# Second layer's vertical recursion on quarter arrays, and another strip order in the last layer

## Time and profile before

| | |
|---|---|
| time, 3 runs | 12891.12 us (12890.92 to 12896.08) |
| the profiled execution's own time | 12888.75 us |
| its span | 12887.0 us |
| PE busy | 12308.6 us (96%) |
| DVE, ACT, POOL busy | 8055.8, 5432.1, 4649.4 us |
| TensorE clock granted | 0.981 of full speed on average |
| layer 0, second stage, matmuls | 1371 to 2409 us |
| layer 1 vertical, matmuls | 2449 to 3776 us |
| layer 1 horizontal, matmuls | 3824 to 5154 us |
| layer 3, matmuls | 9649 to 12878 us |

### The profile page before, as it was taken

The page is one execution under the profiler, slowest core; times in us unless marked ns, Lnnn a source line. Parts: engine busy times, 40 slices in busy tenths (PEclk is TensorE's granted clock), DMA queues, the critical chain, the costliest instruction groups (busy, mean ns, idle before and its releaser), DMA issues. The chain is left out here.

```text
span 12887.0 us, 315788 instructions
## 1 busy us (share of the span) xinstructions
PE 12308.6 (96%) x126170; PEld 8518.5 (66%) x126170; DVE 8055.8 (63%) x17482; ACT 5432.1 (42%) x11157; POOL 4649.4 (36%) x3557
## 2 busy tenths in 40 slices
PE   7999999899989999899999999999989999999998
PEld 6877444577767777455555555555558887787777
DVE  0000677533335544688888888888877777777777
ACT  0000111211213333455555555555546766676666
POOL 0000222100000055566666666666643433334343
PEclk9999999999999999899999999999999999999999
DMA  4333456883765587666666666666642222222222
GB/s 127 135 131 132 132 152 160 158 158 70 153 125 157 151 211 206 94 89 87 88 88 89 87 88 89 88 88 88 89 88 49 50 55 49 52 54 51 52 52 47
DMA packets 2310007, 1323.92 MB, mean 103 GB/s; under 512 B 1872228, under 2 KB 2219867, under 8 KB 2222959
## 3 DMA queue, kind: packets, MB, share of 16 engines
q1 hardware_dynamic: 2041484, 1201.47, 47.0%
q10 hardware_dynamic: 267232, 104.65, 3.4%
HBM read 648.72 MB, written 450.74 MB: 85 GB/s over the span
## 5 line engine op out<-in xcount | busy, mean ns | idle before, releaser
L1583 PE MATMUL l_m<-l_wa,l_pix 128*128 128x288 f32 x8192 | 2211.5, 413 | 12.8 <-DMA l_left<-k_rim_dram 12.8
L1583 PEld LDWEIGHTS l_m<-l_wa,l_pix 128*128 128x128 f32 x8192 | 1475.5, 190 | 698.9 <-issue 375.4
L1439 POOL TENSOR_TENSOR l_qkv<-l_qkv,l_copies 128x576 f32<-128x576 f32 x1024 | 1437.4, 1404 | 633.6 <-DVE l_qkv L1775 633.6
L1429 POOL TENSOR_TENSOR l_pix<-l_raw 128x516 f32<-128x516 f32 x1024 | 1216.7, 1188 | 1043.6 <-DVE l_t L1812 1018.1
L1285 PE MATMUL l1h_ps<-l1h_ring,l1h_w 96*96 96x256 f32 x6120 | 1326.5, 379 | 51.2 <-ACT l1h_ring L1233 47.6
L1056 PE MATMUL l1v_ps<-l1v_rows,l1v_w 96*96 96x256 f32 x6120 | 1326.4, 378 | 31.1 <-ACT l1v_rows L1029 31.1
L2093 PEld LDWEIGHTS l_e<-k_ident,l_turn 128*112 128x112 f32 x9900 | 1086.3, 135 | 248.9 <-issue 126.0
L1285 PEld LDWEIGHTS l1h_ps<-l1h_ring,l1h_w 96*96 96x96 f32 x6120 | 998.6, 163 | 379.1 <-issue 48.0
L2093 PE MATMUL l_e<-k_ident,l_turn 128*112 128x128 f32 x9900 | 1164.3, 276 | 86.2 <-DVE l_out L2255 80.0
L1056 PEld LDWEIGHTS l1v_ps<-l1v_rows,l1v_w 96*96 96x96 f32 x6120 | 990.7, 162 | 366.5 <-issue 30.1
L1269 POOL TENSOR_TENSOR l1h_columns<-l1h_blocks,l1h_ring 96x2048 f32<-96x2048 f32 x64 | 356.2, 5588 | 2418.5 <-DVE l1h_ring L1318 2418.5
(11 more groups left out here) (245 smaller groups left out, 21890.5 us busy)
## 6 DMA issues: line engine op xcount, KB each, us to landing
l0a_x<-x_px_dram SPq DMA_DIRECT2D x128, 1176.0 KB, 5.1
l0b_x<-x_in_dram SPq DMA_DIRECT2D x128, 493.8 KB
l_raw<-l_raw SPq DMA_DIRECT2D x128, 483.6 KB, 7.2
l_raw<-x_dram SPq DMA_DIRECT2D x1280, 48.0 KB, 3.7
l_x<-x3p_dram SPq DMA_DIRECT2D x132, 384.0 KB
l_out<-x_dram SPq DMA_DIRECT2D x528, 96.0 KB
out_dram<-l_out SPq DMA_DIRECT2D x132, 384.0 KB
x_dram<-l0b_out ACTq DMA_DIRECT2D x256, 193.5 KB, 3.1
```

The source lines that it names most:

```text
L1429: nc.gpsimd.tensor_tensor(pix[:, n % 2, i, half * HALF:(half + 1) * HALF].rearrange("p (r w) -> p r w", w=PW), in0, in1, op).then_inc(pix_ ...
L1439: nc.gpsimd.tensor_tensor(q, q, copies[:, g % 2, 1:2, :].broadcast_to([128, 2, OUTC]), ALU.add)\
L1583: last = nc.tensor.matmul(bank[i][:, 0:OUTC], pix[:, k, i, first:first + 128], wa[:, b, i, :], start=True, stop=(i in (1, 2)))
```

## The change

1. **Layout.** `x1` is in natural column order (DVE's L910 and L916 write and read contiguously; ACT's copy reads 16 columns at a time).
2. **Vertical recursion.** A row of two images is kept in one of two layouts, by its parity. *Whole* (even rows): one image on partitions 0 to 47, the other on 64 to 111, 256 columns each. *Parted* (odd rows): the left column half of both images on partitions 0 to 47, the right half on 64 to 111, each half 130 columns wide, so that two columns are computed twice. A matmul takes its input from one side and writes to one side of PSUM, so a whole row gives a parted one and the reverse, with no copy. Each of the 5 taps is a 48x48 matrix, and per tap there are 4 matmuls, one for each quarter of the array, of 130 columns (from a whole row) or 128 (from a parted one). `ps[g]` has two banks, one for each input side. A step-group is thus 20 matmuls of the code in place of 3. DVE still does one instruction, on 112 partitions by 260 or 256 elements.
3. **Way up.** The result of row h is written over row h - 1 (`place`), so that layouts still alternate. At the turn ACT and POOL copy the last row into the whole layout, ten increments of `kept`, and PE waits for them.
4. **Copies and DMAs.** DVE and POOL clear the slots before the first load (8 and 4 of them). A chunk is loaded in 12 DMAs in place of 8 and saved in 4 in place of 4. On the way up ACT copies the whole rows and half of the parted ones, POOL the other half. The constants are loaded behind the first chunk.
5. **Layer 3.** POOL's strip copy (L2315) also waits until all four pieces of its unit are gated. With j = 1 DVE does piece 3 after the residuals.

```diff
@@ stage_l0_apply, DVE
-    place = out[:, kk, 2*n:2*n+2, 1:W+1].rearrange("p r (q u) -> p r u q", q=2)
+    place = out[:, kk, 2*n:2*n+2, 1:W+1]
@@ stage_l1_vertical
+    TAPS, HALO = 5, 2
+    RH = CH // 2
+    PART = HW2 + HALO
+    whole = sb("whole", [PP, SL, GI, RH, W + 2 * HALO])
+    parted = sb("parted", [PP, SL, GI, RH, 2, PART + 2 * HALO])
+    def place(n):  return n if n <= LAST else 2 * LAST - n - 1
+    def source(n): return n - 1 if n <= LAST else 2 * LAST - n
@@ tensor
     for n in range(1, STEPS + 1):
         for g in range(2):
...
+            elif n == LAST + 1:
+                pe.wait_ge(state[g], n - 1)
+                pe.wait_ge(kept, 10)
             else:
                 pe.wait_ge(state[g], n - 1)
-            for s in range(3):
-                last = nc.tensor.matmul(ps[g][0:C2, 0:GI * HW2], w[:, s, :],
-                    X[:, before // CH % SL, g*GI:(g+1)*GI, before % CH, s:s + HW2], start=(s == 0), stop=(s == 2))
-            last.then_inc(product[g], 1)
+            for t in range(TAPS):
+                for r in range(2):
+                    for c in range(2):
+                        if at % 2 == 0:
+                            first = t + c * (W - PART)
+                            x, width = whole[side(r), k, g, row, first:first + PART], PART
+                        else:
+                            first = t + 2 * r
+                            x, width = parted[side(r), k, g, row, c, first:first + HW2], HW2
+                        last = nc.tensor.matmul(ps[g][side(c), r, 0:width], w[side(r), t, :], x,
+                                                start=(t == 0), stop=(t == TAPS - 1), skip_group_check=True)
+                        if t == TAPS - 1:
+                            last.then_inc(product[g], 1)
@@ vector
-    dve.wait_ge(product[g], n)
+    dve.wait_ge(product[g], 4 * n)
     nc.vector.scalar_tensor_tensor(out=x, in0=ps[g][0:PP, :, 0:(HW2 if at >= 0 and at % 2 == 0 else PART)], ...
@@ gpsimd (new), way up
+    for g in range(2):
+        pool.wait_ge(state[g], up_step(c * CH))
+        for i in range(2):
+            for q in range(2):
+                turn_parted(nc.gpsimd.tensor_copy, c, 1, g, i, q).then_inc(turned_low, 1)
@@ stage_l3, DVE
                     if not (first and j == 0) and (j < 2 or last):
-                        for piece in (2, 3):
-                            gated(n if j else n - 1, j - 1 if j else 2, piece)
+                        gated(n if j else n - 1, j - 1 if j else 2, 2)
+                        if j != 1:
+                            gated(n if j else n - 1, j - 1 if j else 2, 3)
                     if j < 2 and not first:
                         for s in range(2):
                             residual(n, j, s)
+                    if j == 1:
+                        gated(n, 0, 3)
@@ stage_l3, POOL
                     pool.wait_ge(added, u + 1)
+                    pool.wait_ge(gate_out, u * 4 + 4)
                     nc.gpsimd.tensor_copy(strip[:, j], inner(4)).then_inc(saved, 1)
```

More of the change, by code:

```diff
@@ L916, in _ @@
                             nc.vector.tensor_tensor(
[L917 removed]
+                                place, bank[2 * n + 1][0:O, :].rearrange("p (r w) -> p r w", r=2), place,
                                 ALU.add).then_inc(added, 1)
@@ L998, in store_up @@
             def store_up(c):
                 k = c % 2
-                sp.wait_ge(turned, 2 * B * (NCH - c))
+                sp.wait_ge(turned, 12 * (NCH - c))
+                sp.wait_ge(turned_low, 8 * (NCH - c))
                 for i in range(B):
[L1002 to L1005, removed]
-                          .then_inc(stored[k], 16)
@@ L1019, in _, with rows_of_parted, turn_parted @@
             for k in range(2):
-                sp.wait_ge(stored[k], 128 * (NCH // 2))
+                sp.wait_ge(stored[k], 192 * (NCH // 2))
+        def rows_of_parted(c):
+            yield parted[:, c % SL, :, 0:RH - 1, :, :], HALO, slice(1, RH)
+            if c > 0:
+                yield parted[:, (c - 1) % SL, :, RH - 1:RH, :, :], HALO, slice(0, 1)
+            else:
+                yield keep[:].rearrange("p g (o i) w -> p g o i w", o=1), 0, slice(0, 1)
+        def turn_parted(copy, c, h, g, i, q):
+            for rows, margin, into in rows_of_parted(c):
+                first = margin + 2 * h
+                src = rows[side(h), g, :, i, first:first + HW2].rearrange("p v (n u q) -> p q n v u", n=WBLK // 2, q=2)
+                last = copy(turn_p[side(h), c % 2, g, i, :, q, into, :], src[:, q])
+            return last
@@ L1031, in _ @@
             for g in range(2):
                 act.wait_ge(state[g], LAST)
-                nc.scalar.activation(keep[:, g * GI:(g + 1) * GI, :],
-                                     X[:, SL - 1, g * GI:(g + 1) * GI, CH - 1, 1:HW2 + 1], ACT.Copy).then_inc(kept, 1)
+                for h in range(2):
+                    at = HALO + 2 * h
+                    copy(whole[side(h), SL - 1, g, RH - 1, HALO + h * HW2:HALO + (h + 1) * HW2],
+                         parted[side(h), SL - 1, g, RH - 1, h, at:at + HW2]).then_inc(kept, 1)
@@ L1035, in _ @@
+                copy(keep[:, g], parted[:, SL - 1, g, RH - 1, :, HALO:HALO + PART]).then_inc(kept, 1)
             for c in range(NCH - 1, -1, -1):
                 if c < NCH - 2:
[L1037 to L1043, removed]
+                    act.wait_ge(stored[c % 2], 192 * ((NCH - 1 - c) // 2))
@@ L1062, in _ @@
         @block.vector
         def _(dve):
[L1064 to L1068, removed]
+            nc.vector.memset(gn_w[:], 0.0)
+            nc.vector.memset(gn_p[:], 0.0)
+            for g in range(2):
+                last = nc.vector.memset(ps[g][32:HI, :, 0:PART], 0.0)
```

191 lines of the change are left out of this document (129 added, 62 removed).

## The result

The changed kernel takes 13168.26 us (median of 4 runs, 13157.29 to 13184.52) against 12891.02 us before: a ratio of 1.0217, 95% interval 1.0199 to 1.0234. It is 277 us slower, where 86 us faster was forecast. The profiled execution took 13184.52 us, its span is 13181.4 us.

A forecast was written before the change was run, and what follows sets the result against it. Vertical stage taken as bound by columns through PE, after the change by instruction packets. Terms -19 + 4 - 3 - 68 = -86 us; 12888.75 - 86 = 12803, the runs' median 2.4 above: 12805 us, range 12615 to 12950.

The forecast's parts named there:

- The vertical steps: Vertical stage: 319 instruction packets at 4.10 us each set the pace, 1307 us against 1326, so -19 us.
- DMA load doesn't seem to matter: Vertical stage: time per instruction packet taken as independent of DMA share: 4.24 us at 0.15, 4.37 at 0.02, 3.86 at 0.53.
- The price without load: PE's instruction stream, vertical stage: 4.10 us per packet of 256 instructions, bounds 3.86 and 4.45.
- the first rival: Vertical stage: instructions come in time and columns set the pace, -204 us there, kernel 12620 us; chance 0.15.
- The second rival: Vertical stage: instruction stream still slower with DMAs beside it, 4.77 us a packet, +128 us, kernel 13019 us; chance 0.12.
- DVE, ACT, POOL: Vertical stage: their work and DMA stay hidden behind PE's time, DVE's instruction 0.49 us, all at nothing.
- Edges: Vertical stage's start, turn and end: 0, +2 and +2, sum +4 us, bounds -3 and +12.
- Layer 0: DVE's add, made contiguous, may be 0.35 us shorter but off the path save at image ends: -3 us (0 to -6).
- Layer 3: With the strip copy after the fourth gate, the first gate takes 0.68 us, not 1.53: -68 us, bounds -90 and -20.
- the three terms: Layer 3, gain per unit: 0.83 us with j = 0, 0.25 with j = 1, 0 with j = 2.

The follow-up runs named there:

- the wait alone: The kernel before, with only the edit that makes POOL's strip copy in layer 3 wait for the gate's last pieces: 12748.88 us, ratio 0.9883.

## Why the prediction was wrong

- **The vertical steps** failed: forecast -19, bounds -95 and +93, measured +429. The count was right (319 packets). The failed step is "DMA load doesn't seem to matter". It rested on three stretches of 4 us in the earlier trace rows, the busiest at a share of 0.53, from a stage whose mean share is 0.23; the vertical stage stood at 0.66 in the earlier trace rows and at 0.90 in the last line of the earlier trace rows. I compared shares inside one quiet stage and carried the result to a busy one. The stage's own load was the thing to bound, and no row bounded it. In its place the runs show that the stage's transfers decide: 3.69 us a packet with the transfers cut, 5.5 with them, 8.8 at full input load.
- **The price without load** was too high, not too low: 3.69 us a packet against the 4.10 taken and the 3.86 called the lowest. I took layer 3's packets for a limit of delivery; they also had ACT, DVE and the wait for them in between, and how much of the 3.86 to 5.08 is which, no run separates. Without load the first rival, instructions in time, is nearly right: 12563.84 measured, 12620 worked out. That is closer than its terms: the stage took 1178 us against 1122, and layer 3 gained 153 us against 68.
- **The second rival** had the right mechanism, "with DMAs beside them", and 0.12 of the chance. It stopped at 4.77 us a packet, since its range was made of layer 3's 4.45 and 5.08; the stage went to 5.5.
- **The clock** had no term, in the stage or in layer 3. In the stage it is at most 200 of the 602 us.
- **The range** was added up wrong at its upper end: +93 + 4 - 3 - 20 on the median gives 12965, not 12950. The measured 13168 lies outside either.
- **DVE, ACT, POOL** hidden: right. DVE 484 and 489 ns, waiting for PE. **Edges** +10 against +4, inside the bounds. **Layer 0** -4 against -3: DVE's add fell from 1073 to 691 ns, 0.38 us where 0.35 was expected, and it was hidden, as said.
- **Layer 3** had the right mechanism and half the size: -140 against -68, outside its bounds of -90 and -20. The gates fell to 681 ns as forecast. Cut at each unit's first convolution matmul, the units with j = 0, 1, 2 took 1033.6, 914.9 and 1239.4 us in all before and 959.6, 872.4 and 1217.7 us in the changed kernel: 1.12, 0.64 and 0.33 us a slab, 2.1 in all, where the forecast had 0.83, 0.25 and 0. So each of the three terms was too small. With j = 0 the median unit gained 0.86 us, as forecast, and the mean more: these units spent 75 us at half clock before and 7 now. With j = 1, I gave 0.25 us, since DVE would wait for the projection. DVE in fact comes to that residual late because its gates were slow, as the wait alone shows by shortening the residual's wait by 33 us. With j = 2, I had 0; 12 of its 22 us are shorter waits of PE, mostly for "issue", and why is open.
- The Trainium skill's rule for such pairs ("SBUF — State Buffer", "SBUF: two separate sides") is that a DVE instruction with two SBUF inputs and a GpSimd one that reads SBUF take the shared ports in turn, whole instructions at a time. 894 against 682 ns with the copy moved agrees in the main. By the rule, a gate that starts 0.05 us after a copy of 1.04 us would end 1.67 us after its start, an estimate from the earlier trace rows and that rule; it took 1.53.
- "Mostly hidden", as the Trainium skill has instruction fetching ("Runtime: NRT & Kernel Launch", "Instruction fetch mechanics"), holds here without transfers (1178 us, 1.00 of the clock) and not with them.

## What to carry to other kernels

Count the instructions that TensorE must fetch for each us of work, and read the DMA share of the very stage in which it must fetch them: here 69 a us came without transfers and 29 beside full loads. The clock falls with the stops, but don't add its loss to theirs before you have seen whether the stop-to-stop distance changes with it. If the work repeats, put it in a hardware loop over fixed tiles, of no more instructions than are held (1280 were, here), and let idle engines carry the data to and from them. And before an operand's price is carried from one stage to another, ask in which respect the two differ most; here it was the one respect that the forecast dismissed.

## What the runs showed of the hardware

- TensorE gets through 16 KB of instructions in 3.7 us without transfers and in 8.8 us at full input load (2455 to 2504 us).
- Under that load the packets came 9.8 us apart whether TensorE ran at full clock between two stops or at half.
- A loop of 1280 instructions is held, one of 1920 isn't, one of 1600 was once and once not. A loop that isn't held costs more than no loop (2036 and 1968 us against 1758).
- Reads of 16 KB packets did more harm to the stream at a share of 0.38 (230 us) than 256-byte writes at 0.45 (70 us), one run each.
